# Second layer's experts: 72 packed float32 blocks of 256 slots against 40 fixed blocks of 512 slots in two float16 parts

## What is computed

```python
E, K, CF, I = 8, 2, 1.25, 512
N = Bx * Cx                        # 8192 tokens
cap = int(N * K * CF / E)          # 2560 slots per expert
logits = x @ Wg.T
top_v, top_i = jax.lax.top_k(logits, K)
gates = jax.nn.softmax(top_v, axis=-1)
...
exp_batches = jnp.zeros((E, cap, d)).at[flat_e, pos_safe].set(x[tok], mode='drop')
h = jnp.einsum('ecd,edf->ecf', exp_batches, W1)      # d = 256, f = 1024
inp, gate = jnp.split(h, 2, axis=-1)
h = jax.nn.gelu(inp, approximate=False) * gate
exp_out = jnp.einsum('eci,eid->ecd', h, W2)
gathered = exp_out[flat_e, jnp.minimum(pos_safe, cap - 1)]
out = jax.ops.segment_sum(jnp.where(keep, gates_f, 0.0)[:, None] * gathered, tok, num_segments=N)
```

## Time and profile before

| what | us |
|---|---|
| median of 3 runs | 5096.67 |
| lowest and highest | 5091.45, 5097.61 |
| profiled execution, its own time | 5088.36 |
| its span in the trace | 5086.6 |
| PE busy | 4492.6 (88%) |
| DVE busy | 4103.5 (81%) |
| ACT busy | 3533.4 (69%) |
| POOL busy | 1682.3 (33%) |
| stage of the tables, start (first DMA issued) | 1682.1 |
| experts, first and last product of PE | 1698.8, 2499.8 |
| attention, first product | 2513.8 |

### The profile page before, as it was taken

The page is one execution under the profiler, slowest core; times in us unless marked ns, Lnnn a source line. Parts: engine busy times, 40 slices in busy tenths (PEclk is TensorE's granted clock), DMA queues, the critical chain, the costliest instruction groups (busy, mean ns, idle before and its releaser), DMA issues. The chain is left out here.

```text
span 5086.6 us, 90731 instructions
## 1 busy us (share of the span) xinstructions
PE 4492.6 (88%) x32649; PEld 2026.2 (40%) x32649; DVE 4103.5 (81%) x4837; ACT 3533.4 (69%) x6199; POOL 1682.3 (33%) x1155
## 2 busy tenths in 40 slices
PE   5778778777776699999899998999998999999998
PEld 3225225224223588888622222222222222222225
DVE  5997998898898332322399998999998999999996
ACT  5765766666663111111399998999998999999993
POOL 1883883883884322222211111021111211121003
PEclk8998998998998899999999999999999999999998
DMA  2402601201201655555311112121112211222016
GB/s 82 155 1 100 199 1 62 71 1 41 76 1 63 194 184 185 190 192 194 100 34 40 35 34 51 35 53 34 41 35 50 52 41 35 51 52 70 22 28 187
DMA packets 333697, 390.74 MB, mean 77 GB/s; under 512 B 172019, under 2 KB 288590, under 8 KB 322446
## 3 DMA queue, kind: packets, MB, share of 16 engines
q0 software_dynamic: 42784, 208.59, 12.6%
q1 hardware_dynamic: 286174, 174.18, 12.5%
q10 hardware_dynamic: 4352, 2.66, 0.2%
HBM read 248.78 MB, written 137.57 MB: 76 GB/s over the span
## 5 line engine op out<-in xcount | busy, mean ns | idle before, releaser
L1661 DVE TENSOR_REDUCE at_mpart<-at_ps 128x1 f32<-128x1024 f32 x2048 | 2348.1, 1211 | 87.8 <-PE at_ps L1550 55.5
L1646 ACT ACTIVATE at_E<-at_ps 128x512 f32<-128x512 f32 x4096 | 2222.3, 594 | 159.5 <-PE at_ps L1565 73.3
L1572 PE MATMUL at_ps<-at_E,at_vst 128*32 128x256 f32 x16400 | 1312.4, 391 | 24.7 <-ACT at_osb L1627 20.9
L1550 PE MATMUL at_ps<-at_ks,at_qs 48*128 48x512 f16 x4096 | 800.0, 387 | 51.8 <-DMA at_qs<-at_mrow 25.4
L1565 PE MATMUL at_ps<-at_qs,at_ks 50*128 50x512 f16 x4096 | 789.8, 382 | 21.6 <-ACT at_E L1646 20.7
L1434 POOL DMA_INDIRECT at_y<-yd,at_gidx x128 | 129.4, 1011 | 1662.5 <-DVE at_mx L1666 1581.0
L890 POOL TENSOR_TENSOR l_work<-l_work 128x1024 f32<-128x1024 f32 x256 | 604.3, 2361 | 78.7 <-DVE l_work L899 70.3
L1358 ACT ACTIVATE at_late<-at_ps 128x256 f32<-128x256 f32 x288 | 110.6, 384 | 638.9 <-PE at_ps L1301 638.9
L1572 PEld LDWEIGHTS at_ps<-at_E,at_vst 128*32 128x32 f32 x16400 | 326.4, 108 | 562.7 <-issue 412.5
L786 PE MATMUL l_ps<-l_bc,l_sel 96*128 96x512 bf16 x1024 | 313.3, 395 | 268.5 <-DVE l_work L899 126.7
L1550 PEld LDWEIGHTS at_ps<-at_ks,at_qs 48*128 48x128 f16 x4096 | 196.3, 92 | 870.3 <-DVE at_mpart L1661 451.5
(11 more groups left out here) (261 smaller groups left out, 4212.2 us busy)
## 6 DMA issues: line engine op xcount, KB each, us to landing
xd<-l_zero SPq DMA_DIRECT2D x4, 5120.0 KB, 33.7
yd<-l_zero SPq DMA_DIRECT2D x4, 5120.0 KB, 33.5
at_qs<-qp SPq DMA_DIRECT2D x132, 128.0 KB
at_ks<-kp SPq DMA_DIRECT2D x396, 32.0 KB
ot<-at_osb SPq DMA_DIRECT2D x516, 17.0 KB
at_qs<-qp SPq DMA_DIRECT2D x132, 64.0 KB
at_vst<-vp SPq DMA_DIRECT2D x65, 128.0 KB, 4.6
at_qs<-at_mrow SPq DMA_DIRECT2D x516, 2.0 KB
```

What stands on the lines that cost most here:

```text
L1550: mm = pe.matmul(ring[n % 2][:, r, :], m.qs[row, buf, bass.ts(i, P)], m.ks[row, buf, bass.ts(kh, BANK)], start=True, stop=True)
L1572: mm = pe.matmul(O[32 * q:32 * q + 32, :], m.vst[:, par, SLOTS_A * kk + sl, :], m.E[:, sl % 4, kk, bass.ts(q, QG)], start=(sl == 0 and kk ...
L1646: act.activation(m.E[:, sl % 4, kk, bass.ts(hf, BANK)], S[chunk(sl, 2 * hf + kk) % 3], ACT.Exp, scale=scale).then_inc(s.ex, 1)
L1661: dve.tensor_reduce(m.mpart[:, job:job + 1], ring[n % 2].rearrange("p a b -> p (a b)"), AX_X, ALU.max).then_inc(s.ring_free, 1)
```

## The change

It replaces how the second layer's experts are computed; the routing, the slots and what is read from `yd` stay.

- **Blocks.** All slots of all experts are worked on, in 40 fixed blocks of 512 slots, five for each expert (`PER`). No list of blocks is made: `totals`, `blk`, `lane` and the gathers go, and rows and results move by direct DMAs of 512 KB (`load_rows`, `rows_out`). `yd` is no longer filled with zeros.
- **Two float16 parts.** A float32 operand is replaced by a high float16 part and a low one, the rest. A product is three float16 products: high by high, high by low, low by high. Weights are scaled by powers of two: ACT squares them (`squares`), PE sums the squares by column with ones (`norms`), DVE makes the factors (`scales`), ACT writes the high parts (`weights_high`) and DVE the low ones (`weights_low`). This is done once per expert, during the previous expert's blocks 1, 2 and 3. The weights in float32 have one buffer (`wst`), their parts have two (`wparts`). Rows and hidden values are cut the same way in each block (`rows_high`, `rows_low`, `hidden_high`, `hidden_low`).
- **Order.** A block on PE is: hidden 0 and 1, first half of the next block's transposition, hidden 2, second half, hidden 3, and then the output products of the block before. DVE's evacuation of these (`results`, 1024 columns) stands at the end of its block too, ahead of the peaks' reductions. POOL stores a block when its results are out, and issues the next load of rows behind that store.
- **Peaks** stand in blocks 4 to 19, two in each. The first expert's preparation stands ahead of DVE's constants.

The diff, cut to this:

```diff
@@ constants
-ROWS = 256
-BLOCKS = CAP // ROWS
-PACKED = 2 * T // ROWS + E1
-WBUFS = 3
+ROWS = 512
+PER = CAP // ROWS
+BLOCKS = E1 * PER
@@ scan_batch, SyncE
-                if b < 2:
-                    blank = (io.xd, io.yd)[b]
+                if b == 0:
...
@@ list_blocks becomes mix_factor
+                load_weights(sp, io, m, 0)
...
+                for n in range(2):
+                    load_rows(sp, io, m, n)
@@ run_experts, GpSimd
-                rows_in(0)
-                weights(0)
-                weights(1)
-                for n in range(PACKED):
-                    if n + 1 < PACKED:
-                        if n:
-                            pool.wait_ge(s.turned, n)
-                        rows_in(n + 1)
-                    if n + 2 < PACKED:
-                        if n:
-                            pool.wait_ge(s.out, n)
-                        weights(n + 2)
+                for n in range(BLOCKS):
+                    e = n // PER + 1
+                    if n % PER == 0 and e < E1:
+                        pool.wait_ge(s.wlo, 2 * e)
+                        load_weights(pool, io, m, e)
+                    if 1 <= n < BLOCKS - 1:
+                        pool.wait_ge(s.turned, KD * n)
+                        load_rows(pool, io, m, n + 1)
                     if n:
                         rows_out(n - 1)
@@ run_experts, TensorE
+                def norms(e, n):
+                    pe.wait_ge(s.squares, e + 1)
+                    if peaks_before(n):
+                        pe.wait_ge(a.ring_free, peaks_before(n))
...
+                    for c in range(2 * KD):
+                        pe.matmul(FIRST[:, 0, :], m.ones, m.wsq[:, bass.ts(c, BANK)], start=(c == 0), stop=(c == 2 * KD - 1))
...
+                def hidden(n, mt):
+                    w, x = n // PER % 2, n % 2
+                    for half in range(2):
+                        i = MT * n + mt
+                        if half == 0 and i >= 2:
+                            pe.wait_ge(s.prod, i - 1)
+                        if half == 1 and i >= 1:
+                            pe.wait_ge(s.gelu, i)
+                        for k in range(KD):
+                            col = 2 * I1 * k + I1 * half + P * mt
+                            for wpart, xpart in ((0, 0), (0, 1), (1, 0)):
+                                mm = pe.matmul(hid_bank(n, mt, half), m.wparts[:, w, wpart, col:col + P], m.xt[:, x, xpart, k, :],
...
-                for n in range(PACKED):
-                    pe.wait_ge(wl[n % WBUFS], 16 * (n // WBUFS + 1))
-                    pe.wait_ge(s.xt, n + 1)
-                    for mt in range(4):
-                        hidden(n, mt)
-                    if n + 1 < PACKED:
-                        turn(n + 1)
-                    if first_peak(n) is not None:
-                        peak(first_peak(n))
...
-                    outputs(n)
+                for n in range(BLOCKS):
+                    e = n // PER
+                    if n % PER == 0:
+                        pe.wait_ge(s.wlo, 2 * (e + 1))
+                    pe.wait_ge(s.xlo, KD * (n + 1))
+                    hidden(n, 0)
+                    hidden(n, 1)
+                    if n + 1 < BLOCKS:
+                        turn(n + 1, 0)
+                    hidden(n, 2)
+                    if n + 1 < BLOCKS:
+                        turn(n + 1, 1)
+                    hidden(n, 3)
+                    if n:
+                        outputs(n - 1)
+                    for job in peaks(n):
...
+                        peak(job)
...
+                    if n % PER == PREPARE and e + 1 < E1:
+                        norms(e + 1, n + 1)
+                outputs(BLOCKS - 1)
@@ run_experts, VectorE
+                scales(0)
+                weights_low(0)
+                for k in range(KD):
+                    rows_low(0, k)
                 dve.memset(m.one3, 1.0)
...
+                for n in range(BLOCKS):
+                    for mt in range(MT):
+                        product(n, mt)
+                        if mt:
+                            hidden_low(n, mt - 1)
+                        if mt == 1 and n + 1 < BLOCKS:
+                            rows_low(n + 1, 0)
+                        if mt == 2 and n + 1 < BLOCKS:
+                            rows_low(n + 1, 1)
+                    hidden_low(n, MT - 1)
+                    if n:
+                        results(n - 1)
                     first_peaks(n)
...
+                    if n % PER == PREPARE and e + 1 < E1:
+                        scales(e + 1)
+                    if n % PER == DIVIDE and e + 1 < E1:
+                        weights_low(e + 1)
+                results(BLOCKS - 1)
```

More of the change, by code:

```diff
@@ new lines, in turn @@
+                def turn(n, k):
+                    if k == 0 and n < 2:
+                        pe.wait_ge((io.x_first0, io.x_first1)[n], 16)
+                    elif k == 0:
+                        pe.wait_ge(xl[n % 2], 16 * (n // 2))
+                    if KD * n + k:
+                        pe.wait_ge(s.xlo, KD * n + k)
+                    for r in range(RT):
+                        mm = pe.transpose(TURN[:, bass.ts(r, P)], m.xin[:, n % 2, r, bass.ts(k, P)], m.ident)
+                    mm.then_inc(s.turned, 1)
@@ new lines, in weights_high, with rows_high @@
+                def weights_high(e):
+                    act.wait_ge(s.scales, e + 1)
+                    if e >= 2:
+                        act.wait_ge(s.out, PER * (e - 1))
+                    for part, at in ((W1, A1), (W2, A2)):
+                        act.activation(m.wparts[:, e % 2, 0, part], m.wst[:, part], ACT.Copy, scale=factor(e, at)).then_inc(s.whi, 1)
+                def rows_high(n, k):
+                    act.wait_ge(s.turned, KD * n + k + 1)
+                    if n >= 2:
+                        act.wait_ge(s.hid, 2 * MT * (n - 1))
+                    act.activation(m.xt[:, n % 2, 0, k, :], TURN, ACT.Copy, scale=2.0 ** X_EXP).then_inc(s.xhi, 1)
@@ new lines, in gelu, with hidden_high @@
+                def gelu(n, mt):
+                    i = MT * n + mt
+                    act.wait_ge(s.hid, 2 * i + 1)
+                    if i >= 2:
+                        act.wait_ge(s.prod, i - 1)
+                    act.activation(m.g[:, mt % 2, :], hid_bank(n, mt, 0), ACT.Gelu, scale=factor(n // PER, IA)).then_inc(s.gelu, 1)
+                def hidden_high(n, mt):
+                    act.wait_ge(s.prod, MT * n + mt + 1)
+                    if n >= 2:
+                        act.wait_ge(s.out, n - 1)
+                    act.copy(m.ht[:, n % 2, 0, mt, :], m.h[:, mt % 2, :]).then_inc(s.hhi, 1)
@@ L1369, in first_peaks, with results @@
+                def results(n):
+                    if n >= 2:
+                        dve.wait_ge(st[n % 2], 16 * (n // 2))
+                    dve.wait_ge(s.out, n + 1)
+                    dve.tensor_scalar(m.yout[:, n % 2, :, :].rearrange("p r d -> p (r d)"), m.pair[3].rearrange("p b d -> p (b d)"), factor(n // PER, IY), None, ALU.mult).then_inc(s.y, 1)
                 def first_peaks(n):
-                    job = first_peak(n)
-                    if job is not None:
+                    for job in peaks(n):
@@ L1890, in build @@
     with ExitStack() as ctx:
[L1891 removed]
+        kept = {n: ctx.enter_context(nc.semaphore(n)) for n in ("scattered", "w_first", "x_first0", "x_first1", "wg0", "xg0", "xg1", "yg0", "yg1")}
         score_scale = ctx.enter_context(nc.sbuf_tensor("score_scale", [P, 1], F32))[:]
```

254 lines of the change are left out of this document (132 added, 122 removed).

## The result

The changed kernel took 5148.07 us in the median (5132.43 to 5152.14, 4 runs), the kernel before beside it 5094.66 us (5091.45 to 5097.61, 4 runs). The ratio is 1.0099, with a 95% interval of 1.0077 to 1.0122: **about 1% slower, some 50 us**. The forecast was no change, 5096. The time lies near the upper end of the range and beside rival 4's 5150, in which the clock falls at the many short waits.

A forecast was written before the change was run, and what follows sets the result against it. PE's work bounds the experts' stage. With 120 us less multiplication PE would end at 2382, plus 52 (peaks), 15 (norms), 46 (rows) and 4 (clock) = 2499, against 2500 before; forecast 5096 us, range 5060 to 5150.

The forecast's parts named there:

- rival 4: PE's clock falls at the many short waits: 2.1 us after each of up to 35, 40 to 73 more, 5150; chance 0.08.
- the clock: PE in the experts' stage: the clock starts low after the two long waits, 2.1 us each, 4 in all.
- Price of a product, block work: PE: 16-bit products take 0.216 us at 512 columns, 0.108 at 256; a block 16.45 us, 40 blocks 658 against 778 before.
- rivals 3 and 5: 3: output products' weight loads show, 179 us more, 5275, chance 0.06; 5: 512-column products paced at 0.131 us, 4933, chance 0.02.
- Start: Start of the experts' stage: first hidden product at 1713.6; PE then waits for DVE's memsets and first product until 1728.5.
- Peaks: Two peak pairs behind the outputs in blocks 4 to 19: PE goes on at T + 3.25, 16 x 3.25 = 52 us.
- T: The moment when PE could start something else behind a block's output products; later steps are timed from it.
- Norms: Norms of the next expert, seven times: 9 us of work, 4 for second reductions, 2 for the maxima's transposition; 15 in sum.
- Rows: Next block's rows load behind POOL's store: 15 waits of 1.4 us, 21, and six behind weights, 25; sum 46 us.
- Rival 1: Rows land early, at or before T + 5.2: the 15 waits vanish, 28 us less, 5068; chance 0.17.
- Rival 2: Rows land late through POOL's queue: 21 us per us of lateness, decides from T + 7.0, 5138 at T + 8.5; chance 0.15.
- Attention and output: The attention behind the experts isn't touched by the change, and the way out is the same; attention starts near 2513.

## Why the prediction was wrong, step by step

**The failing step** is the clock: "After the two long waits the clock starts low, 2.1 each: 4", with 2.1 for the start. These 6 us were 40. The other terms of the sum came out within 4 us, the rows' by errors that cancel:

- *Price of a product, block work.* 0.109 per output product and 0.216 per hidden one, 16.47 us per block against 16.45. Weight loads stay hidden: rivals 3 and 5 are out. The Trainium skill's 0.131 us for a sustained stream (TensorE: Matmul & The Clock Gate, Back-to-back issue gap) doesn't show here: 12 of the 1920 products of 512 columns take 2193.05 - 2190.46 = 2.59 us, 0.216 each. That is its N/2.4 + 2.5 ns, which it gives for the gap of a single product.
- *Start.* First hidden product at 1714.47 (1713.6 forecast), restart at 1729.12 (1728.5). Right: the mixing factor was ready at 1695.7, 2.1 us later than before (2 forecast), and ACT's first squares began at 1696.67 (1696.7); from there to the first product it took 17.8 us for 16.9.
- *Peaks.* T is 2007.64 + 5.24 = 2012.88, and the hidden products go on at 2015.95: 3.07 us against 3.25, in all 16 blocks; 49 for 52.
- *Norms.* 9.1 of work, 5.1 and 1.5 of waits: 15.7 for 15.
- *Rows.* 49.3 for 46, by the mechanism described, but the nearness of the sums is in part luck. POOL's two issues behind the results at the end of block 21, from its timeline; then PE's wait that follows them, and one of the two long ones, where weights stand between:

```profile
2184.78 0.54 POOL L1240 DMA_DIRECT2D yd<-at_late  x1 [17.34 <-DVE at_late L1470]
2185.30 0.53 POOL L1101 DMA_DIRECT2D at_late<-xd  x1
```

```profile
2182.93 5.34 PE L1294 MATMUL at_ps<-at_late,at_wparts 128*128 128x512 f16 x24
2189.97 0.66 PE L1280 MATMUL at_ps<-at_ident,at_late 128*128 128x128 f32 x4 [1.70 <-DMA at_late<-xd]
...
2349.16 1.12 PE L1280 MATMUL at_ps<-at_ident,at_late 128*128 128x128 f32 x4 [6.28 <-DMA at_late<-xd]
2350.07 4.15 PE L1294 MATMUL at_ps<-at_late,at_wparts 128*128 128x512 f16 x12
```

T is 2182.93 here: the load is issued at T + 2.37 (2.4 forecast), the rows are there at T + 7.0 (6.5), the wait is 1.70 (1.4). Rival 1 is out. Rival 2 was to decide from T + 7.0 on, so the rows came to its edge. The 15 short waits were 27.8 us for 21. Five more weren't foreseen (2.6 us: blocks 2, 22, 27 and 32, where the norms covered most of the wait but not all, and one behind block 13), which is why there are 26 and not 21. The six behind weights were 18.9 for 25: the two long ones held (6.13 and 6.28 for 6.3), but behind blocks 4, 9, 14 and 19 PE waited 1.4 to 2.2 us for 3.1, since the hidden products ahead of the wait ran 1.2 to 1.7 us longer at the half clock and came to it later. So the clock's loss hid a part of the rows'.

- *End.* The last outputs wait 1.5 us for the results before them, which the sum didn't have.
- *Attention and output.* Forecast as untouched, measured 8.5 us longer: 1.3 ahead of the first step, 3.3 in the first 48, 2.1 in the last 80, 1.8 behind them. The first two go with more time at half clock, whose cause is open; the others are within what executions of one kernel differ by.

The sum of the errors: 34 (clock), 3.3 (rows), 1.5 (end), 0.7 (norms), 0.6 (start), less 2.9 (peaks) is 37, and PE's end was missed by 2536.8 - 2499.5 (the forecast's sum before rounding) = 37.3.

**Why the clock's term failed.** Rival 4 had the right mechanism, and a chance of 0.08. Its price of 40 to 73 us more was somewhat high, where 34 more were measured: in the changed kernel's trace the clock fell behind 13 of the 16 waits at the peaks and both long waits for rows, but from 2160 us on behind only 2 (1.95 and 2.60 us) of the 16 shorter waits for rows. That its 5150 meets the median is in part luck, since 8.5 of the 44.1 us of the profiled executions arose behind the experts. It was held down with "short waits in the scan left it at 9". But a digit 9 is a mean over 127 us that reads 0.90 or more: the scan from 560 to 900 us, with its waits, stands at 0.94, and the changed kernel, which lost 40 us, shows 9 as well. None of the rows that the prediction went by has a wait of 2 us that comes back in every block of dense products. The sum then charged the clock for the two waits over 5 us alone, and 36 us of waits of 2.3 us were taken to cost nothing beyond their length. The stage before ran at 1.00 because PE never stopped there; a change that makes it stop over 40 times gives that up.

## What to carry to other kernels

A wait of the engine that sets the time is to be counted twice: once for its length, and for TensorE once more for the products behind it at half clock, here 0.2 to 0.5 of the waits' length when they recur in every block of 16 to 20 us. When a step moves to the end of a loop's body, look at what is issued behind it on the queues of other engines: here the load of rows moved to the block's end with the store in front of it, and one line (the rows asked for a block earlier) mended that for 66 to 68 us. And fill a wait with busy products to learn its hidden price before working to remove it.

## What was not expected of the hardware

- Work that nobody reads made the kernel faster: 16 x 10 products in the place of 2.26 us waits gave 12 to 21 us, and the granted clock of that stretch rose from 0.92 to 0.98.
- The same wait isn't followed by the same clock: behind 2.26 us, 24 products took 5.35 us in 3 of 16 blocks and 6.5 to 7.9 in the others, and the stretch stood at 0.92 in the mean. What decides between them no run here shows.
- Waits of 1.7 us alone, filled in the same way, gave only 5 us of clock for 28 us of waits, about half the rate of those of 2.26 us and of the long ones.
